# Score products of two pairs of heads in five tasks in place of six, and three orders of work changed

## The reference, cut to what matters

```
xn = _layernorm(x, axis=-1)
qkv = xn @ qkv_w + qkv_b                       # q, k, v: 32 heads of 16
q = _rope(q, cos, sin); k = _rope(k, cos, sin)
scores = jnp.einsum('bqhd,bkhd->bhqk', q, k) * scale
scores = scores + (1.0 - causal) * MASK_VAL
probs = jax.nn.softmax(scores, axis=-1)
ctx = jnp.einsum('bhqk,bkhd->bqhd', probs, v)
s = ctx @ out_w + out_b
g = silu((silu(xn @ W_gate.T) * (xn @ W_up.T)) @ W_down.T)
x = x + s * g                                  # then block 1
```

## Time and profile before

| | |
|---|---|
| median of 3 runs (lowest, highest) | 634.31 us (631.81, 635.22) |
| the profiled execution | 631.3 us |
| its span, first to last instruction | 629.4 us |
| granted TensorE clock | 0.998 of full speed |
| PE, DVE, ACT, POOL busy | 605.8, 382.3, 300.0, 384.5 us |
| slots of batch 0, of batch 1 begin at | 38.2 us, 255.5 us |
| slot 47 (the last score task) of each begins at | 163.8 us, 381.1 us |

### The profile page before, as it was taken

How to read it: one execution, slowest core, us unless ns; L and a number is a source line. 1 busy time by engine, 2 the same in 40 slices (tenths; PEclk the granted TensorE clock), 3 DMA queues, 4 the chain that set the end, 5 groups by cost and what they waited for, 6 DMA issues and landing times.

```text
span 629.4 us, 9886 instructions
## 1 busy us (share of the span) xinstructions
PE 605.8 (96%) x3368; PEld 419.6 (67%) x3368; DVE 382.3 (61%) x908; ACT 300.0 (48%) x476; POOL 384.5 (61%) x598
## 2 busy tenths in 40 slices
PE   6998999999999999799999999999999999999996
PEld 5765565666567888565656665687888676867664
DVE  5958768666426596687586663264986261516257
ACT  3646658555644623467574556445122344232432
POOL 7787757654434677767585554346888585731264
PEclk9999999999999999999999999999999999999999
DMA  8798756754422336667568734734430000000002
GB/s 294 234 302 260 224 158 166 196 141 102 110 79 80 89 100 180 195 203 232 142 193 248 192 94 140 295 106 148 151 120 1 1 1 1 0 1 1 0 34 101
DMA packets 60370, 83.64 MB, mean 133 GB/s; under 512 B 17936, under 2 KB 26768, under 8 KB 60320
## 3 DMA queue, kind: packets, MB, share of 16 engines
q1 hardware_dynamic: 57392, 73.70, 39.9%
q10 hardware_dynamic: 2928, 9.31, 4.1%
HBM read 65.17 MB, written 26.99 MB: 146 GB/s over the span
## 4 chain that ended last, share of the span: by engine, by line
PE 50%; ACT 2%; DVE 2%; POOL 2%; issue 1%; ACTq 0%; POOLq 0%; DVEq 0%
PE proj_ps L958 4%; PE proj_ps L1163 3%; PE proj_ps L1164 3%; PE ctx_ps L1115 3%; PE proj_ps L959 3%; PE proj_ps L960 3%; PE score_ps L988 2%; PE ctx_ps L1163 2%; PE scoreT_ps L1163 2%; PE ctx_ps L1164 2%; PE scoreT_ps L1164 2%; PE scoreT_ps L997 2%; PE one_turn_ps L1242 1%; POOL hsL L933 1%; PE proj_ps L1170 1%; PE score_ps L1262 1%
## 5 line engine op out<-in xcount | busy, mean ns | idle before, releaser
L772 POOL TENSOR_TENSOR w_lo<-raw,w_hi 128x512 fp32r<-128x512 f32 x98 | 133.6, 1367 | 68.3 <-ACT w_hi L1328 62.8
L1516 DVE CUSTOM_DVE_ANT_0 score_ps<-score_ps,causal 128x512 f32<-128x512 f32 (+3 forms) x256 | 119.4, 518 | 65.4 <-PE score_ps L988 65.2
L1372 ACT ACTIVATE probs_T<-scoreT_ps 128x1024 f32<-128x1024 f32 (+1 forms) x96 | 84.7, 882 | 67.0 <-PE scoreT_ps L997 66.1
L958 PE MATMUL proj_ps<-xn_hi,w_hi 128*128 128x512 f32 x224 | 99.8, 445 | 1.6 <-ACT by_sin L1306 1.2
L959 PE MATMUL proj_ps<-xn_hi,w_lo 128*128 128x512 f32 x224 | 88.2, 394 | 0.0
L960 PE MATMUL proj_ps<-xn_lo,w_hi 128*128 128x512 f32 x224 | 87.9, 393 | 0.0
L770 POOL TENSOR_SCALAR w_hi<-raw 128x512 fp32r<-128x512 f32 x50 | 34.1, 681 | 41.7 <-PE proj_ps L960 37.3
L958 PEld LDWEIGHTS proj_ps<-xn_hi,w_hi 128*128 128x128 f32 x224 | 42.0, 187 | 26.4 <-issue 11.6
L806 POOL TENSOR_SCALAR_AFFINE_SELECT probs_T<-probs_T 128x256 f32<-128x256 f32 x128 | 52.3, 428 | 11.4 <-ACT probs_T L1372 11.4
L933 POOL TENSOR_TENSOR hsL<-hidden_T,hsH 128x256 fp32r<-128x256 f32 x44 | 38.0, 880 | 26.7 <-ACT hsH L1457 26.2
L988 PEld LDWEIGHTS score_ps<-k_st,q_st 50*128 50x128 f32 x256 | 21.6, 184 | 46.8 <-issue 25.4
(11 more groups left out here) (314 smaller groups left out, 1345.9 us busy)
## 6 DMA issues: line engine op xcount, KB each, us to landing
raw<-w SPq DMA_DIRECT2D x98, 256.0 KB, 3.0
rows<-rows_hi SPq DMA_DIRECT2D x32, 256.0 KB, 3.8
arranged<-tern SPq DMA_DIRECT2D x96, 85.0 KB
q_st<-rows SPq DMA_DIRECT2D x32, 200.0 KB
k_st<-rows SPq DMA_DIRECT2D x32, 200.0 KB
rows<-rows_lo SPq DMA_DIRECT2D x16, 256.0 KB, 4.6
gate_w<-arranged ACTq DMA_DIRECT2D x4, 704.0 KB, 7.2
up_w<-arranged ACTq DMA_DIRECT2D x4, 704.0 KB, 7.8
```

Of the source, the lines that this page charges most:

```text
L772: nc.gpsimd.tensor_tensor(w_lo[n % SPLIT][:, :], raw[n % RAW][:, :], F32(w_hi[n % SPLIT][:, :]), ALU.subtract).then_inc(unit_ready, 1)
L958: nc.tensor.matmul(acc, lh, rh, start=first, stop=False)
L1372: nc.scalar.activation(probs_T[gp % 4][:, c:c + 2 * w].rearrange("p (h c) -> p h c", h=2), scoreT_ps[:, :, 0:w], ACT.Exp, scale=0.25).then ...
L1516: m = nc.vector.tensor_tensor_reduce(out=block, in0=block, in1=causal[:, S - w:], scale=1.0, scalar=-3e38, op0=ALU.add, op1=ALU.max, accum ...
```

## The change

Two pairs of heads are handled together in five tasks, each with 512 columns for each head. Tasks 0 and 1 are the first pair's as before, tasks 3 and 4 the second pair's, and task 2 holds the 256-column blocks of both pairs. A batch has 40 score tasks in place of 48 and 45 slots with triples in place of 53. The maxima of the two pairs are joined and turned in slots 5g + 3 and 5g + 5; the context products stand in slots 11 + 5g to 14 + 5g, the context's turn in 16 + 5g. Group g's stack is wanted in slot 5g; the read of a later group stands in slot 5g - 5, that of group 2 in slot 8 as before. Exponentials always take 1024 columns, and `probs_T` has a tile for each task, five for a group, with two groups of buffers. The arrangement copies are spread over 36 slots.

Three orders of work change beside that: the four weight loads L1418 go from ACT's queue to SP's, behind the last arrangement copy and waits for all ropes and the last context product; the magnitude product L1049 goes behind the first four blocks of V; and in batch 0 DVE's bias sums go behind the ropes of batch 1.

```
-A_TILES = [[(3, 0)], [(2, 0), (0, 384)], [(1, 0)]]
-B_TILES = [[(0, 0)], [(1, 0), (3, 384)], [(2, 0)]]
-WIDTH = (512, 512, 256)
-TASKS = 3 * PAIRS
+A_TILES = [[(0, 3, 0)], [(0, 2, 0), (0, 0, 384)], [(0, 1, 0), (1, 1, 256)], [(1, 3, 0)], [(1, 2, 0), (1, 0, 384)]]
+B_TILES = [[(0, 0, 0)], [(0, 1, 0), (0, 3, 384)], [(0, 2, 0), (1, 2, 256)], [(1, 0, 0)], [(1, 1, 0), (1, 3, 384)]]
+PARTS = 5
+TASKS = PARTS * GROUPS
...
 def read_in(s):
-    return next((g for g in range(1, GROUPS) if (1 if g == 1 else max(6 * g - 6, unit_slot(K_UNIT[g // 2]) + 7)) == s), None)
+    return next((g for g in range(1, GROUPS) if (1 if g == 1 else max(PARTS * g - 5, unit_slot(K_UNIT[g // 2]) + 7)) == s), None)
...
 def max_in(s):
-    j = s // 3 - 1
-    return j if s % 3 == 0 and 0 <= j < PAIRS else None
+    g, x = divmod(s, PARTS)
+    j = {3: 2 * g, 0: 2 * g - 1}.get(x, -1)
+    return j if 0 <= j < PAIRS else None
...
 def pv_in(s):
-    g, kt = divmod(s - 12, 6)
+    g, kt = divmod(s - 11, PARTS)
...
 def ctx_in(s):
-    return (s - 17) // 6 if s >= 17 and (s - 17) % 6 == 0 ...
+    return (s - 16) // PARTS if s >= 16 and (s - 16) % PARTS == 0 ...
...
 def copies_in(b, s):
-    at = [9 + 43 * n // COPIES[b] for n in range(COPIES[b])]
+    at = [9 + 36 * n // COPIES[b] for n in range(COPIES[b])]
...
     # sync
             sp.wait_ge(arranged, 16 * len(ARRANGE))
+            sp.wait_ge(turned_ready, 8 * B)
+            sp.wait_ge(pv_done, GROUPS * B)
+            for dst, src in ((w1T[:, :, :], A["w1T"]), (w2T[:, :, :, :], A["w2T"]), (woT[:, :], A["woT"]), (bout[:, :], ...)):
+                sp.dma_start(dst, src).then_inc(small1_in, 16)
             sp.wait_ge(out_used, KC * B)
...
     # tensor
-            def scores(b, j, x):
-                for part, (qt, c) in enumerate(A_TILES[x]):
+            def scores(b, g, x):
+                for part, (i, qt, c) in enumerate(A_TILES[x]):
                     for hh in range(2):
-                        q, k = stacks(b, j, hh)
+                        q, k = stacks(b, 2 * g + i, hh)
...
-                if b == 0:
-                    pe.wait_ge(ones_set, 2)
-                    pe.wait_ge(asum_ready, 3)
-                    nc.tensor.matmul(proj_ps[1][:, 0:3], V[:, 0, 0:P], abs_sums[:, :], ...).then_inc(tot_ready, 1)
-                else:
+                if b:
                     pe.wait_ge(combined, 2 * NT * (b - 1) + NT)
                 for kc in range(KC):
+                    if b == 0 and kc == 1:
+                        ...    # the same product
...
-                        if x == 0:
-                            pe.wait_ge(*copied(b, ("max", j)))
+                        if x in (0, 2):
+                            pe.wait_ge(*copied(b, ("max", 2 * g + x // 2)))
...
     # scalar
-                        nc.scalar.activation(probs_T[gp % 4][:, c:c + 2 * w].rearrange("p (h c) -> p h c", h=2), scoreT_ps[:, :, 0:w], ACT.Exp,
+                        nc.scalar.activation(probs_T[g % 2][x][:, :, :], scoreT_ps[:, :, :], ACT.Exp, scale=0.25)...
...
-                    if b == B - 1 and s == LAST_DOWN - 2:
-                        for dst, src in ((w1T[:, :, :], A["w1T"]), ...):
-                            act.dma_start(dst, src).then_inc(small1_in, 16)
...
     # vector
+            def bias_sums(b):
+                for x, i in enumerate(OUT_TILES):
+                    dve.wait_ge(bias_step, 2 * NT * b + x + 1)
+                    nc.vector.scalar_tensor_tensor(out=X[:, i, :], in0=down_tanh[i][:, :], scalar=0.25, in1=X[:, i, :], ...)
...
-                for x, i in enumerate(OUT_TILES):      # the bias sums, for both batches
+                if b == B - 1:
+                    bias_sums(b)
                 ...                                    # the gate products, L1702
                 if b < B - 1:
                     first_ropes(b + 1)
+                    bias_sums(b)
                 ...                                    # the last sums, L1708
```

More of the change, by code:

```diff
@@ L75, with block_at @@
 NORM_STATS, NORM_ROWS, NORM_TURN = SCORE_SLOTS + 3, SCORE_SLOTS + 5, SCORE_SLOTS + 7
-def t_col(hh, kt):
-    x = (0, 1, 2, 1)[kt]
-    return sum(2 * w for w in WIDTH[:x]) + WIDTH[x] * hh + (384 if kt == 3 else 0)
+def block_at(i, kt):
+    return next((x, c) for x, blocks in enumerate(B_TILES) for i0, kt0, c in blocks if (i0, kt0) == (i, kt))
 def triple_slot(k):
@@ L340, in program @@
     o_pt = at[0]
-    probs_T = [sb("probs_T0", [P, 2560], f32, offset=o_pt0)] + [sb(f"probs_T{n}", [P, 2560], f32) for n in range(1, 4)]
+    probs_T = [[sb(f"probs_T{n}{x}", [P, 2, 512], f32, offset=o_pt0 + 4096 * x if n == 0 and x < 3 else o_pt + 4096 * (PARTS * n + x - 3))
+                for x in range(PARTS)] for n in range(2)]
+    at[0] += 30720
+    max_cols = sb("max_cols", [P, 2, NT, 34], f32r)
     o_h = at[0]
@@ L743, in _ @@
             sp.wait_ge(arranged, 16 * len(ARRANGE))
+            sp.wait_ge(turned_ready, 8 * B)
+            sp.wait_ge(pv_done, GROUPS * B)
+            for dst, src in ((w1T[:, :, :], A["w1T"]), (w2T[:, :, :, :], A["w2T"]), (woT[:, :], A["woT"]), (bout[:, :], A["bout"].partition_broadcast(P))):
+                sp.dma_start(dst, src).then_inc(small1_in, 16)
             sp.wait_ge(out_used, KC * B)
@@ L797, in keep_causal @@
             def keep_causal(b, s):
[L799 to L803, removed]
+                g, x = prob_in(s)
                 pool.wait_ge(probs_ready, TASKS * b + s - LAG + 1)
-                for _, c in B_TILES[x]:
-                    m = nc.gpsimd.affine_select(out=halves[:, :, c:c + P], in_=halves[:, :, c:c + P], pattern=[[0, 2], [1, P]],
-                                                compare_op=ALU.is_ge, fill=0.0, base=0, channel_multiplier=-1)
+                for _, _, c in B_TILES[x]:
+                    block = probs_T[g % 2][x][:, :, c:c + P]
+                    m = nc.gpsimd.affine_select(out=block, in_=block, pattern=[[0, 2], [1, P]], compare_op=ALU.is_ge, fill=0.0,
+                                                base=0, channel_multiplier=-1)
                 m.then_inc(probs_masked, 1)
@@ L990, in scores, with scores_T @@
                 m.then_inc(score_done, 1)
-            def scores_T(b, j, x):
-                for part, (kt, c) in enumerate(B_TILES[x]):
+            def scores_T(b, g, x):
+                for part, (i, kt, c) in enumerate(B_TILES[x]):
                     for hh in range(2):
-                        q, k = stacks(b, j, hh)
+                        q, k = stacks(b, 2 * g + i, hh)
                         m = nc.tensor.matmul(scoreT_ps[:, hh, c:c + S - kt * P], k[:, kt * P:(kt + 1) * P], q[:, kt * P:],
@@ L1045, in _ @@
                         job_part(b, u, kc)
-                if b == 0:
-                    pe.wait_ge(ones_set, 2)
-                    pe.wait_ge(asum_ready, 3)
-                    nc.tensor.matmul(proj_ps[1][:, 0:3], V[:, 0, 0:P], abs_sums[:, :], start=True, stop=True).then_inc(tot_ready, 1)
-                else:
+                if b:
                     pe.wait_ge(combined, 2 * NT * (b - 1) + NT)
                 for kc in range(KC):
+                    if b == 0 and kc == 1:
+                        pe.wait_ge(ones_set, 2)
+                        pe.wait_ge(asum_ready, 3)
+                        nc.tensor.matmul(proj_ps[1][:, 0:3], V[:, 0, 0:P], abs_sums[:, :], start=True, stop=True).then_inc(tot_ready, 1)
                     pe.wait_ge(unit_ready, UNITS * b + V_UNIT + kc + 1)
@@ L1507, in row_maxima @@
             def row_maxima(b, s):
-                j, x = score_in(s)
+                g, x = score_in(s)
                 dve.wait_ge(score_done, TASKS * b + s + 1)
-                if x == 0 and PAIRS * b + j >= 2:
+                j = 2 * g + x // 2
+                if x in (0, 2) and PAIRS * b + j >= 2:
                     dve.wait_ge(max_ready, PAIRS * b + j - 1)
-                for qt, c in A_TILES[x]:
+                for i, qt, c in A_TILES[x]:
                     w = (qt + 1) * P
@@ L1610, in first_ropes @@
                     rope_second(b, u)
+            def bias_sums(b):
+                for x, i in enumerate(OUT_TILES):
+                    dve.wait_ge(bias_step, 2 * NT * b + x + 1)
+                    nc.vector.scalar_tensor_tensor(out=X[:, i, :], in0=down_tanh[i][:, :], scalar=0.25, in1=X[:, i, :],
+                                                   op0=ALU.mult, op1=ALU.add).then_inc(bias_step, 1)
             for t in range(NT):
```

56 lines of the change are left out of this document (23 added, 33 removed).

## The result

The changed kernel takes 628.78 us (median of 6 runs, 626.57 to 630.2) against 634.32 of the kernel before (6 runs): a ratio of 0.9918, 95% interval 0.9894 to 0.9942, 5.5 us less where 7.1 were forecast. The profiled execution took 628.73 us with a span of 626.8; that of the kernel before took 631.3 with 629.4, so the two spans lie only 2.6 us apart.

The account below looks back on a forecast made before the run. PE was taken to bound the kernel, busy 605.8 of 629.4 us. Terms -7.6 + 0 + 3.2 + 0.5 - 1.7 - 1.5 gave -7.1 us, so 627.2 from a median of 634.3; 8-in-10 range 621.5 to 633.

Parts of the forecast that it names:

- PE's own work: Score stages on PE: merged half tasks save 4.6 us and fewer slots 3.0, together -7.6 us.
- maxima: PE's waits for DVE's row maxima in the score slots: 4.5 us before and after, so 0.
- stack of group 2: Slot 10 of each batch: loads landing in 7.0 us make PE wait 1.6 us anew, +3.2 us.
- ACT: ACT's order: new waits of +2.8 us at slot 20's rope copies, old jams of 1.2 and 1.1 gone; net +0.5 us.
- (a): Batch 0's bias sums behind batch 1's ropes: PE's wait at slot 0 of batch 1 goes, -1.7 us.
- (b): Four weight loads leave ACT's queue, where they held `w_hi` and `ctx_hi` and through them PE: -1.5 us.
- (c): Magnitude product behind four V products: PE's 0.7 us wait is hidden, but slot 0 awaits its stacks, so 0.
- the price of the mixed task: Score stages: a mixed task costs 0.34 us (transposed 0.33) against two halves of 0.22 (0.26), saving 4.6 us.
- The turn in slot 21: Context turn on PE, held up by ACT's rope copies of slot 20: a wait of 1.4 us, +2.8 in two batches.
- the hand-made timetable of DVE: DVE followed through the first slots, ropes between maxima: 2.4 us of PE waiting in a batch, as now.
- Rival C: Context turn waits for the maxima's bank in every group, 0.8 us per turn: +12.8 us, 640.0; chance 0.08.

Follow-up runs that it names:

- orders alone: The kernel before with only the three changed orders of work (magnitude product, four weight loads, bias sums): 627.87 us, ratio 0.9917.
- Loads back: The kernel of second units early with the four weight loads of block 1 on ACT's queue again: 625.39 us, ratio 0.9882 to the kernel before.
- bias sums alone: The kernel before with only batch 0's bias sums moved behind the ropes of batch 1: 629.59 us, ratio 0.9942.
- context turn later: The changed kernel with the context's turn one slot later: 635.52 us, ratio 1.0044 to the kernel before.
- stack late: The kernel of second units early with group 2's read in SP's slot 8 instead of 7: 626.02 us, ratio 0.9886 to the kernel before.
- second units early: The changed kernel with one more triple ahead of slot 0 and unit 8's first rope products a slot earlier: 623.39 us, ratio 0.9848.

## Why the prediction came out nearly right

The table splits the spans of the profiled executions, 629.4 and 626.8, by the forecast's own terms, in us. "Measured" compares before, orders alone and the changed kernel stage by stage. "Products of DVE" are PE's waits until DVE has worked up a unit (`gate_silu`).

| term | forecast | measured |
|---|---|---|
| PE's own work | -7.6 | -7.3 |
| maxima; products of DVE | 0 | +0.6; +1.2 |
| stack of group 2 | +3.2 | +4.9 |
| ACT | +0.5 | -0.7 |
| bias sums (a), loads (b), magnitude (c) | -1.7, -1.5, 0 | -2.3, -1.6, not told apart |
| half clock | none | +1.7 |
| rest: pace of matmuls, stretch ahead of batch 1, others | none | +0.9 |
| sum | -7.1 | -2.6 |

**PE's own work** was right, and with it the price of the mixed task. Score stages less PE's waits and the lost clock are 137.7 us in both batches of orders alone, 133.4 and 133.7 in the changed kernel; of these 8.3 us 0.5 in each batch come back behind the slots, where the context turn of group 6 now stands. What I made of it was partly wrong: I set the rows of 0.22 and 0.34 against the Trainium skill's N/2.4 + 2.5 ns ("TensorE: Matmul & The Clock Gate", Back-to-back issue gap). Within a task the trace agrees with the page that columns are what counts (0.34 us for one product of 512 columns a head and for two of 256). Two tasks of 0.22 against one of 0.34 leave 0.1 us that is paid for each task, however many products it has, and that is what the merger saves.

**The stack's term was mis-sized**, by 1.7 us: "The read is issued at 57.91, as slot 8 starts". In the new order SP comes to it 0.95 and 0.73 us behind the slot's start, 0.6 and 0.3 of them spent waiting until the unit's own rows had landed: the slots have become shorter, and the write of the rows is now only just done when they are read. The landing, guessed at 7.0, took 6.76 and 7.62 to PE's start, and slots 8 and 9 last 5.6. In batch 0: 0.95 + 6.76 - 5.59 = 2.12, the wait in the row.

**ACT and DVE.** The turn in slot 21 waits, where I said, but 0.79 in place of 1.4; of the old jams 2.3 us went, as many as I reckoned but not quite the same (0.6 of `by_sin`, 1.1 of `probs_T`, 0.6 of `ctx_sums`). New are waits for `gate_silu`, 1.4 us in place of 0.2, which the hand-made timetable of DVE missed; it had the maxima nearly right. Rival C is out: turns wait in one group only.

**The orders.** (a) brought more than its bound of 1.7: beside the wait at slot 0 another 0.5 us goes from the first units (in the changed kernel that 0.5 is back, 25.09 us from the first unit to slot 0; it stands in the last row but one). Loads back puts (b) at 2.1 us, bias sums alone puts (a) at 2.5 at full clock.

**What was missed altogether** is the clock, on both sides. The forecast added to a span the 3.0 us by which the median of before lies above its profiled run, without asking what they are: at 0.58 us for each 0.001 of clock, the kernel before loses 1.9 us in the mean. With its wait of 1.74 us at slot 0 of batch 1 and that for `ctx_lo` gone, orders alone gains 5.2 us in the means as run where the spans show 3.6. The tasks put two waits of 2 to 3 us in their place, and the changed kernel loses 2.5 us in the mean. At full clock the change is worth 5.1 us. So that 627.2 stands near 628.8 is in good part luck: errors of both signs cancel. The orders were to bring 3.2 us and brought 5.2 as run; the tasks beside the orders were to bring 3.9 and brought 0.3 at full clock and nothing that can be told as run.

The link from wait to fall is shown in two directions: filling the waits brings the clock to 1.000, and one read a slot later lowers the mean clock by 0.0032. What a given wait does is not certain. Of 27 waits of 1.68 us and more in the score stages of all readable profiles 8 had a fall behind them; in the changed kernel's one profiled execution the wait of 1.69 us at slot 3 had one in batch 0 and none in batch 1. The Trainium skill ("TensorE: Matmul & The Clock Gate", Part 1: The HAM clock gate) says that the array's clock depends on how busy it has lately been and is one of two levels; the rows agree: 0.50 in a stretch wholly behind a fall and 1.00 elsewhere, values between them where a change falls into the stretch.

## What to carry to other kernels

When tasks are merged, the work saved is easy to price; list for each producer how much earlier its result is now wanted, and follow the queue that brings it, since the saving ends at the first one that is late. Ask also when the data that the queue is to read have themselves landed. An idle stretch of TensorE can cost more than its length: ask of each wait of 1 us and more, also those that are there already, whether the clock stays up behind it, and look at the clock of every run before putting an offset on a profile. Edits that come in one change want to be run apart: here the three small ones alone gave as much time as all together.

## What the hardware showed that was not expected

- The granted clock falls to half for 3.4 us in the midst of a kernel whose PE is 96% busy. In one profile (context turn later) it stayed down for 10 us. A fall of 3.4 us costs up to 1.7 us, and next to nothing where another engine would have been waited for anyway.
- PE's matmuls have a slightly different pace in kernels with the new tasks. The 48 of the out projection of batch 0 take 10.99 us, 228.9 ns each, in the changed kernel and 10.88, 226.6 ns, in orders alone, and all ten kernels with the new tasks whose traces could be read have 10.98 us or more there (three of them 11.20 in one batch or both). The tiles of weights lie 1088 bytes further on in SBUF since the change, and the transfers beside them differ; neither was tried. The addresses can't be all of it, since stack late (11.20) and second units early (10.99) have the same. Start of the first product of the out projection and of the next stage, in the changed kernel and in orders alone:

```profile
217.93 0.39 PE L962 MATMUL proj_ps<-w_hi,ctx_hi 128*128 128x512 f32 x1
...
228.92 0.39 PE L962 MATMUL score_ps<-xn_hi,w_hi 128*128 128x512 f32 x1
```

```profile
217.61 0.39 PE L962 MATMUL proj_ps<-w_hi,ctx_hi 128*128 128x512 f32 x1
...
228.49 0.39 PE L962 MATMUL score_ps<-xn_hi,w_hi 128*128 128x512 f32 x1
```
